# Polynomial attention by score matrices and Square activations in place of feature expansions, with unused matmuls in the stage

## What is computed

```python
qkv = (x @ Wqkv.T + bqkv).reshape(B, N, 3, H, D)
...
q = q * scale
v1 = jnp.concatenate([jnp.ones((B, H, N, 1), dtype=v.dtype), v], axis=-1)
qn = _normalize(q) * (scale * temperature)
kn = _normalize(k) * scale
vN = v1 / N
kv_mod = jnp.einsum('bhni,bhnj,bhne->bhije', kn, kn, vN)
kv = jnp.einsum('bhnd,bhne->bhde', kn, vN)
vsum = jnp.sum(vN, axis=-2)[:, :, None, :]
y = A * jnp.einsum('bhni,bhnj,bhije->bhne', qn, qn, kv_mod) + scale ** 2 * Bc * jnp.einsum('bhnd,bhde->bhne', qn, kv) + scale ** 4 * Cc * vsum
y_norm, y = (y[..., :1], y[..., 1:])
y = y / y_norm
return out @ Wproj.T + bproj
```

## Time and profile before

| | |
|---|---|
| median of 3 runs | 1999.27 us (1997.89 to 2005.81) |
| profiled execution, its own time | 2006.71 us |
| its span, first to last instruction | 2004.9 us |
| granted TensorE clock, mean over the span | 0.865 of full speed |
| the polynomial attention, in the trace | from 1388.5 us (its constants are set) to 1714.0 us |
| busy over the span | PE 86%, DVE 74%, ACT 38%, POOL 34% |

### The profile page before, as it was taken

The page is one execution under the profiler, slowest core; times in us unless marked ns, Lnnn a source line. Parts: engine busy times, 40 slices in busy tenths (PEclk is TensorE's granted clock), DMA queues, the critical chain, the costliest instruction groups (busy, mean ns, idle before and its releaser), DMA issues. The chain is left out here.

```text
span 2004.9 us, 45616 instructions
## 1 busy us (share of the span) xinstructions
PE 1719.6 (86%) x15064; PEld 1344.4 (67%) x15064; DVE 1488.5 (74%) x4423; ACT 756.6 (38%) x2274; POOL 690.5 (34%) x957
## 2 busy tenths in 40 slices
PE   1499999999769999999999999973999999788887
PEld 1266666666557777777777777752888888677776
DVE  6166676666627898888889888875766665688887
ACT  2245454545324444344344444321222222343442
POOL 2622222222134555545545445532211111322221
PEclk9999999999869999999999999985555555788788
DMA  2000000000000000000000000000000000000000
GB/s 114 1 2 0 0 0 0 0 0 0 1 1 1 1 2 0 0 0 0 0 0 0 0 0 0 1 1 0 1 0 0 0 0 1 1 5 8 4 6 11
DMA packets 6980, 8.13 MB, mean 4 GB/s; under 512 B 6272, under 2 KB 6272, under 8 KB 6784
## 3 DMA queue, kind: packets, MB, share of 16 engines
q1 hardware_dynamic: 6912, 7.25, 1.1%
HBM read 5.71 MB, written 1.54 MB: 4 GB/s over the span
## 5 line engine op out<-in xcount | busy, mean ns | idle before, releaser
L1142 ACT ACTIVATE ex_pT<-ex_T 128x376 f32<-128x376 f32 (+1 forms) x384 | 162.8, 440 | 217.1 <-PE ex_T L1044 207.9
L604 ACT ACTIVATE al_prob<-al_S,al_negmax 94x94 f32<-94x94 f32 (+1 forms) x512 | 146.2, 375 | 180.0 <-DVE al_negmax L731 180.0
L1207 DVE TENSOR_REDUCE ex_negmax<-ex_R 94x2 bf16<-94x376 f32 (+1 forms) x384 | 186.8, 543 | 30.6 <-PE ex_R L1015 30.0
L1044 PE MATMUL ex_T<-ex_qm,ex_kpad 128*128 128x188 f32 x1024 | 189.7, 329 | 0.0
L505 PE MATMUL al_S<-al_kpad,al_qT 128*94 128x376 f32 x384 | 166.5, 516 | 0.0
L1044 PEld LDWEIGHTS ex_T<-ex_qm,ex_kpad 128*128 128x128 f32 x1024 | 163.0, 192 | 5.1
L944 POOL TENSOR_SCALAR_AFFINE_SELECT ex_pT<-ex_pT 128x512 f32<-128x512 f32 x128 | 84.3, 659 | 236.5 <-ACT ex_pT L1142 236.5
L682 POOL TENSOR_TENSOR al_kpad<-al_kT,al_quad_mask 128x1504 f32<-128x1504 f32 x32 | 86.2, 2692 | 186.3 <-ACTq L619 186.3
L731 DVE TENSOR_REDUCE al_negmax<-al_S 94x2 f32<-94x376 f32 (+1 forms) x192 | 99.1, 542 | 62.6 <-PE al_S L506 56.7
L1554 POOL TENSOR_TENSOR ta_kk<-ta_ext 94x320 f32<-94x320 f32 x64 | 60.4, 961 | 246.4 <-DVE ta_qkn L1734 163.0
L1027 PE MATMUL ex_R<-ex_sxT,wsb 128*128 128x188 f32 x256 | 72.3, 364 | 47.5 <-DVE ex_negmax L1207 47.5
(11 more groups left out here) (308 smaller groups left out, 4300.8 us busy)
## 6 DMA issues: line engine op xcount, KB each, us to landing
tok_xin<-x_t SPq DMA_DIRECT2D x4, 760.0 KB, 6.9
wsb<-weights SPq DMA_DIRECT2D x1, 2531.0 KB, 14.2
out<-stream SPq DMA_DIRECT2D x16, 94.0 KB
tok_par<-tok_w SPq DMA_DIRECT2D x1, 4.5 KB, 1.7
```

Source lines behind the costliest of these rows:

```text
L604: last = nc.scalar.activation(p[:, k, cols], S[0:P, k, cols], ACT.Exp, bias=negmax[g % 2][:, m:m + 1])
L1044: last = nc.tensor.matmul(T[:, k, (j % 2) * N:(j % 2 + 1) * N], kpad[par][:, j, 0:K0], qm[e % 2][:], start=True, stop=True)
L1142: nc.scalar.activation(pT[e % 2][rows, k, cols], T[rows, k, cols], ACT.Exp)\
L1207: red(dst, src, AX.X, ALU.max, negate=True).then_inc(sem["r_used"], 1)
```

## The change

`taylor_attention` is written anew. There is no expansion any more: the score matrices themselves are made, head by head, and ACT turns them into weights with one Square.

- Scores (`scores`): for a half of the heads (a group g of 4) PE multiplies k and q, which lie padded to 32 partitions for each head, in 8 calls of 32 rows of the array each (`tile_position=(32 * j, 0)`), into four PSUM banks `T`.
- Weights (`kernel_of`): ACT reads two banks at a time, 94 x 752, and writes Square(T + linear) to `prob`: four such activations for a row.
- `weigh`: PE multiplies `prob` with v (padded to 32 columns), four heads side by side in the array's columns, into `O`; DVE copies it (`oT`); PE picks the 9 columns of each head out and adds the constant part with `flat_part` (16 matmul instructions a row).
- q and k are now transposed on PE (8 calls a row) through one bank `QK`, q first, then, when ACT has copied it, k.
- v is scaled by DVE out of PSUM. The two biases ride as a 65th row of the weights; DVE's two bias additions are gone, and 256 columns of the weight table.
- GpSimd only sets constants (16 operations; before 22, and `kk` for each row). The depth is 5 instead of 8, so 37 steps, and most tiles have one buffer instead of two.
- `keep_busy` issues matmuls that nobody reads (bf16, 128 x 512 columns): 20 of them once, ahead of the third row's first scores, one ahead of each row's transposes of q and k, one ahead of each row's q, k and v.

```diff
-    DIST = TD // 2 + 1
-    F = DIST * TD
...
+    WARM = 20
+    GH = 4
+    G = TH // GH
...
-        CONSTS = 22
-        DEPTH = 8
+        CONSTS = 16
+        DEPTH = 5
...
+            def keep_busy(bank, n):
+
+                for _ in range(n):
+                    nc.tensor.matmul(bank, w_parts[:, 0, 0:128], w_parts[:, 0, 128:640], start=True, stop=True)
+
+            def scores(r, g):
+                u = G * r + g
+                if g == 0:
+                    pe.wait_ge(qk_ready, 2 * (r + 1))
+                need(pe, t_used, u)
+                if isinstance(u, int) and u == 2 * G:
+                    keep_busy(T[:, 0, :], WARM)
+                for s in range(HALVES):
+                    for j in range(GH):
+                        rows = slice(32 * j, 32 * j + 32)
+                        last = nc.tensor.matmul(T[0:P, j, s * N:(s + 1) * N], kT[rows, g, s * P:(s + 1) * P],
+                                                qT[rows, g, :], start=True, stop=True, tile_position=(32 * j, 0),
+                                                skip_group_check=True)
+                last.then_inc(t_full, 1)
...
             def body(t, par):
+                rx, rq, rs, rw, rf = t - 1, t - 2, t - 3, t - 4, t - 5
+                odd = 1 - par
+                if valid(rs):
+                    scores(rs, 0)
+                if valid(rx):
+                    pe.wait_ge(xn_ready, rx + 1)
+                    need(pe, stored, rf)
...
+                if valid(rw):
+                    weigh(rw, par, 1)
+                if valid(rf):
+                    pe.wait_ge(y_ready, rf + 1)
+                    need(pe, stored, rf)
+                    need(pe, xT_ready, upto(rx + 1))
...
+                if valid(rs):
+                    scores(rs, 1)
+                if valid(rw):
+                    pe.wait_ge(o_ready, rw + 1)
...
+                if valid(rq):
+                    pe.wait_ge(qkn_ready, rq + 1)
+                    need(pe, qk_ready, 2 * rq)
+                    keep_busy(QK[:], 1)
+                    for full, first in ((qT_full, 0), (kT_full, G)):
+                        if first:
+                            pe.wait_ge(qk_ready, 2 * rq + 1)
...
+                if valid(rs):
+                    weigh(rs, odd, 0)
+                if valid(rx):
+                    pe.wait_ge(xT_ready, rx + 1)
...
+                    keep_busy(QKV[:], 1)
...
+            def kernel_of(r, g, k):
+                if k == 0:
+                    act.wait_ge(t_full, G * r + g + 1)
+                    need(act, w_full, G * (r - 1) + g + 1)
+                ins = nc.scalar.activation(prob[g][:, 2 * k:2 * k + 2, :], T[0:P, 2 * k:2 * k + 2, 0:HALVES * N],
+                                           ACT.Square, bias=linear[:])
+                if k == 1:
+                    ins.then_inc(t_used, 1)
```

More of the change, by code:

```diff
@@ L1444, in sb, with psum @@
             return ctx.enter_context(nc.sbuf_tensor("ta_" + name, shape, dt))
[L1446 to L1450, removed]
+        def psum(name, shape):
+            return ctx.enter_context(nc.psum_tensor("ta_" + name, shape, F32))
         def sem(name):
@@ L1465, in taylor_attention @@
[L1465 to L1475, removed]
@@ L1480, in taylor_attention @@
+        qkn = sb("qkn", [P, HALVES, 2 * G, GH * PAD_D])
+        qT = sb("qT", [128, G, N])
+        kT = sb("kT", [128, G, N])
+        v1 = [sb(f"v1_{i}", [P, HALVES, TH, PAD_D]) for i in range(2)]
+        prob = [sb(f"prob{i}", [P, GH, HALVES * N]) for i in range(G)]
+        oT = sb("oT", [128, G * N])
+        pick = sb("pick", [128, GH, V1])
+        flat_part = sb("flat_part", [P, P])
+        linear = sb("linear", [P, 1])
         rec = sb("rec", [P, HALVES, TH])
-        y = two("y", [P, HALVES, TH, TD])
@@ new lines, in weigh @@
+            def weigh(r, p, g):
+                pe.wait_ge(t_used, G * r + g + 1)
+                if g == 0:
+                    pe.wait_ge(v_ready, r + 1)
+                need(pe, o_ready, r)
+                for s in range(HALVES):
+                    for j in range(GH):
+                        last = nc.tensor.matmul(O[32 * j:32 * j + 32, g * N:(g + 1) * N], v1[p][:, s, GH * g + j, :],
+                                                prob[g][:, j, s * N:(s + 1) * N], start=(s == 0), stop=(s == 1),
+                                                tile_position=(0, 32 * j), skip_group_check=True)
+                last.then_inc(w_full, 1)
@@ new lines, in body @@
+                if valid(rq):
+                    dve.wait_ge(squares_ready, rq + 1)
+                    need(dve, norm_ready, rq)
+                    nc.vector.tensor_reduce(norm2[:], squares[:].rearrange("p h (a d) -> p (h a) d", d=TD), AX.X, ALU.add)\
+                        .then_inc(norm2_set, 1)
+                if valid(t):
+                    for h in range(HALVES):
+                        last = nc.vector.bn_stats(stats[:, h, :], stream[:, t * HALVES + h, :])
+                    last.then_inc(stats_set, 1)
+                    dve.wait_ge(stats_set, t + 1)
+                    dve.sem_inc(stats_settled, 1)
+                    for h in range(HALVES):
+                        last = nc.vector.bn_aggr(moments[:, h, :], stats[:, h, :])
+                    last.then_inc(var_set, 1)
+                    dve.wait_ge(var_set, t + 1)
+                    nc.vector.tensor_scalar(moments[:, :, 1], moments[:, :, 1], LN_EPS, None, ALU.add)\
+                        .then_inc(moments_ready, 1)
@@ new lines, in body @@
+                if valid(rw):
+                    dve.wait_ge(w_full, G * (rw + 1))
+                    need(dve, y_full, rw)
+                    nc.vector.tensor_copy(oT[:], O[:, 0:G * N]).then_inc(o_ready, 1)
+                if valid(t):
+                    dve.wait_ge(std_ready, t + 1)
+                    nc.vector.reciprocal(rstd[:], std[:]).then_inc(rstd_set, 1)
+                    dve.wait_ge(rstd_set, t + 1)
+                    need(dve, xT_full, t)
+                    for h in range(HALVES):
+                        last = nc.vector.tensor_scalar(xn[:, h, :], stream[:, t * HALVES + h, :], moments[:, h, 0:1],
```

394 lines of the change are left out of this document (142 added, 252 removed).

## The result

| | before | after |
|---|---|---|
| median | 1999.99 us (4 runs, 1997.89 to 2005.81) | 2158.47 us (4 runs, 2157.38 to 2165.2) |
| ratio | | 1.0794, 95% interval 1.0762 to 1.0826 |
| span of the profiled execution | 2004.9 us | 2155.5 us |
| mean granted TensorE clock | 0.865 | 0.848 |
| the stage in the trace | 325.5 us | 480.5 us |

The change costs 158.5 us, 7.9%. The forecast of 2031 us with its range to 2100 missed it; it is rival (c), in which the clock is mostly lost. The two profiled executions differ by less, 150.6 us in span, since the one of the kernel before was itself 6.7 us above its median. In the page of the changed kernel I read the same slices as the earlier trace rows (here 53.9 us each), and the group of the Squares, whose mean of 877 ns is the 0.88 us of the forecast.

The account below looks back on a forecast made before the run. PE bounded the old stage; new rows, 10.0 us from hand-offs at full clock, made 320 us, 343 with clock loss, plus 15.3 for burst, filling and emptying: stage 358, 33 more, median 2031 us, range 1987 to 2100.

Parts of the forecast that it names:

- rival (c): Rewritten stage: clock mostly lost, rows 13 to 15 us, stage 430 to 495, total 2105 to 2170; 0.16 together with (d).
- A row at 2.4 GHz is 10.0 us: Row of the rewritten stage at full clock: 10.0 us, against 9.88 before, with PE working only 6.6.
- At 1.2 GHz 15 us: Row of the rewritten stage at half clock: PE's 13.1 us plus nearly 2 us waiting for the Squares, 15 us.
- the circle: Engines handing one row's pieces to each other, tiles having one buffer: 9.44 us, plus hand-offs 0.4 and array changes 0.15.
- Square of 94 x 752, 0.88 us: ACT's Square with bias out of PSUM, four a row: copy 0.79 plus bias 0.09, 0.88 us each.
- Rival (b): Rewritten stage faster: clock holds and ACT's Squares are cheap; at 0.70 us each, stage 313, total 1987 us; chance 0.10.
- The burst, 6 us: 20 unused matmuls ahead of the third row's scores: 4.4 us at full clock, 8.8 at half, taken as 6.
- Filling and emptying 9.3 us: Time of the stage outside its 32 rows, for filling, emptying and the first row's start: left at about 9.3 us.
- The hole: In each row PE has little to do for over 2 us while ACT does its first two Squares.
- The clock, the step that failed: Rewritten stage at half clock a fifth of the time, so 320 us of rows become 343; chance 0.47 for some loss.
- (d): Burst does not raise the clock: rows start slow, ending in (c) or the forecast, 5 us more; 0.16 together with (c).
- Rival (a): Clock holds throughout the rewritten stage: stage 335 us, total 2009, or 1988 to 2022 with the row's bounds; chance 0.27.

Follow-up runs that it names:

- the last version: Changed kernel with q transposes, `rec` and `y`, root and weighing earlier, moments later, two fillers where PE awaits the first Squares, on-path fillers out: 1971.2 us, ratio 0.9855.

## Why the prediction was wrong

Of its three questions, how long a row is at 2.4 GHz, how long at 1.2, and which of the two the clock does, the first two came out and the third did not.

- **A row at 2.4 GHz is 10.0 us**: 9.91 measured. **At 1.2 GHz 15 us**: 14.95 and 14.85. Both are right in the sum and less so in the parts, and that the parts cancel is luck. PE's own work was put too low: I had 0.67 us for a group of scores or a weighing, and the next instruction starts 0.83 us after the scores (1429.85 to 1430.68) and 0.78 after the weighing (1437.70 to 1438.48). ACT's part of the circle was put too high, by 0.5 us a row: I added up full lengths, but an instruction starts before the last has ended, so the first Square, the root, the second Square and `xT` take 1.98 us (1440.50 to 1442.48), not 2.29, and two Squares in a row 1.66, not 1.76. PE's sum is near 7.9 us at full clock (9.91 less the waits of 1.34 and 0.57 us and about 0.1 for `y`), not 6.6. At half clock it is 13.6 (14.86 less 0.44, 0.57 and 0.22), where I had 13.1 and nearly 2 us of waiting. The Trainium skill (TensorE: Matmul & The Clock Gate, section on packing small matmuls) has a speedup of 3.07 for four row tiles of 512 columns, from which the prediction's estimate of 0.87 us for a group comes. The trace, with 0.83, agrees with it better than with my 0.67.
- **Square of 94 x 752, 0.88 us**: 0.877, out of two plain copies. Rival (b), cheap Squares, is out by the length of a Square, though a Square behind another costs the circle less than that (above). Rows under 9.4 us exist, but by another order of the work.
- **The burst, 6 us**: 5.71. **Filling and emptying 9.3 us**: with the clock held behind both filled holes, 328.4 - 32 x 9.68 = 18.6 us for these and the burst, against 15.3.
- **The hole**: "while ACT does its first two Squares it has little but one weighing and one pair of transposes for over 2 us": seen, with 1.34 us of waiting. The wait for `qT`, 0.57 us, I had only as a link of PE's order and not as a second hole.
- **The clock, the step that failed**: "after a loss the clock should come back, as in the mixture. I take a fifth of the time at half clock". It did not come back: 406 us at 0.50 behind 20.5 us at full. I took the share of time at half clock from the mixture, a stage with other matmuls and other pauses, though no row showed that the new stage would be like it. And I weighed the evidence the wrong way round: this very stage at 0.50 with PE busy for 93% stood in the text as an argument for rival (c), with 0.16 for (c) and (d) together. The kernel without fillers, and the old one with nine, say that it was the strongest evidence at hand: a PE that reads as busy at half clock need not be on its way back to full clock. It can be: with three fillers at each place the clock came back after 58.0 and after 174.1 us.
- **What it cost**: the 406.2 us at 0.50 are the time of some 27 rows at 14.9; at the 10.7 that the forecast's clock gives (343 / 32) they would have taken 113 us less, of the 122 by which the stage passed 358 us. What the other terms were off by comes to some 9 us together.
- **Rival (a)** had the right price for a held clock: stage 335 and total 2009 forecast, 328.4 and 2004.0 measured with both holes filled, which takes seven fillers a row more than the change has. It was the wrong case for the change as made.

The Trainium skill's rule that transposes do not count for the clock (TensorE: Matmul & The Clock Gate, part on PE-mode transposes) stood with rival (c). No run here contradicts it, but none takes the transposes by themselves, and the changed kernel with both holes filled holds the clock with its twelve transposes a row. So it stays open here whether they or the short products left the clock low in the kernel before. (The lists of PE's rows ahead of the prediction leave some calls out: in the trace the row before has the two transposes of `xn` at L1640 as well and eight calls for `Y`, not four, so that sixteen small products are gone and not twelve; the changed row has L1593 and L1610 twice as often as listed, and four calls at L1596.)

Open as well: why the changed kernel kept the clock for 20.5 us and the one with three fillers at each place for 10.2 us once and 99.0 us the next time, with the same row each time. In which moment the clock falls the runs don't tell, nor whether it goes by the emptiest part of a row or by the row as a whole. That it falls less the better the holes are filled, they do.

## What to carry to other kernels

When a change makes PE wait in every row, even for a microsecond, treat the clock as the first term of the sum and not as a correction: cost the kernel at both levels, and give the low one the larger chance if the stage reads 0.50 already while PE reads as busy. Fillers belong where PE waits anyway, right behind the last work before the wait: in the changed kernel they were free there and held the clock, whereas on PE's path they cost their time in each row and held it badly. In the kernel before, where PE was busy for 301.7 of 325.5 us and left hardly a wait to fill, they only cost. Then look at what the waiting engine waits for; an order of small instructions on ACT or DVE that closes a hole pays twice, by its time and by the clock.

## What the runs showed that I had not expected

- PE at half clock for 406 us although the records show it busy for 372 of them. High busy time at half clock can last for a whole stage.
- The same number of fillers, six, gave a stage of 447.7 us in one arrangement (in the longer of its two runs) and 355.4 in another. The Trainium skill (TensorE: Matmul & The Clock Gate, section on a second HAM failure mode) says that short idle moments between groups of matmuls can make the clock go back and forth. The trace agrees: with the q transposes moved and DVE's order left as it was, PE waits 1.4 to 1.5 us for `y` in each row at full clock, and the clock fell and rose eleven times, 10.2 us low each time.
- In the changed kernel the clock was lost in rows in which PE waits 1.34 and 0.57 us and never longer. No long pause is needed. In the last version it waits 0.81 us at one place in each row, and the clock holds.
- With enough fillers the rows raised the clock by themselves: with both holes filled it was up 11 us ahead of the burst.
- Filling the hole made a row at full clock shorter, 9.68 us on average instead of the one row of 9.91 seen without. I expected no change; the cause was not looked for.
- Instructions on 32 rows of the array with weights 94 wide mostly hide their loads: 16 of them pass in 0.83 us at full clock (against 1.3 us, the prediction's bound with one load after another) and in 1.51 at half clock (1600.22 to 1601.73).
